# A one-core transformer block: the expert pipeline one chunk deeper, with four hidden banks and two banks for the rest

## What is computed

```python
h = _layernorm(x) * (1 + ca) + sa
x = x + ga * attn(h)                         # 16 heads of 128, causal
h = _layernorm(x) * (1 + cb) + sb
d = h @ down_w + down_b                      # 256 -> 128
gate, top = top 2 of softmax(h @ router_w + router_b - cost)
out = sum over k, e of gate_k * (gelu(gelu(d * mask_ke) @ w1_e + b1_e) @ w2_e + b2_e)
out = out + 0.1 * (gelu(gelu(d) @ shared_w1 + b) @ shared_w2 + b)
x = x + gb * (out @ up_w + up_b + gelu(h) @ core_w + core_b)
```

## Time and profile before

| | us |
|---|---|
| median of 3 runs | 826.7 (825.47 to 826.98) |
| profiled execution | 826.36 |
| its span, first to last instruction | 824.6 |
| PE busy | 791.6 (96%) |
| DVE busy | 681.7 (83%) |
| ACT busy | 626.6 (76%) |
| POOL busy | 441.8 (54%) |

### The profile page before, as it was taken

The page is one execution under the profiler, slowest core; times in us unless marked ns, Lnnn a source line. Parts: engine busy times, 40 slices in busy tenths (PEclk is TensorE's granted clock), DMA queues, the critical chain, the costliest instruction groups (busy, mean ns, idle before and its releaser), DMA issues.

```text
span 824.6 us, 14456 instructions
## 1 busy us (share of the span) xinstructions
PE 791.6 (96%) x4806; PEld 707.2 (86%) x4806; DVE 681.7 (83%) x1654; ACT 626.6 (76%) x1409; POOL 441.8 (54%) x306
## 2 busy tenths in 40 slices
PE   8899899999999999999999999999998788989997
PEld 7689898999999999999999999999998677768786
DVE  4789998888888888888888888889898898777876
ACT  3787878788778888778887788887778666677873
POOL 2555365644545566544566544675454364848554
PEclk8999999999999999999999999999999899999999
DMA  7263233442233433332233442244232220121121
GB/s 249 74 168 72 64 82 91 105 106 65 64 76 84 112 95 90 74 83 69 64 91 90 102 110 65 64 110 115 65 69 60 70 91 14 65 64 65 65 96 60
DMA packets 47594, 70.55 MB, mean 86 GB/s; under 512 B 5536, under 2 KB 38464, under 8 KB 47392
## 3 DMA queue, kind: packets, MB, share of 16 engines
q1 hardware_dynamic: 47008, 68.81, 31.4%
q0 software_dynamic: 368, 0.81, 0.3%
q10 hardware_dynamic: 144, 0.00, 0.0%
HBM read 25.49 MB, written 2.17 MB: 34 GB/s over the span
## 4 chain that ended last, share of the span: by engine, by line
PE 63%; ACT 15%; DVE 10%; issue 6%; POOL 4%; DMA 1%; POOLq 0%; SPq 0%; DVEq 0%; ACTq 0%
PE M L719 9%; PE M L720 9%; PE M L718 9%; PE T L718 6%; PE T L720 6%; PE T L719 6%; PE S L718 5%; PE S L720 5%; PE S L719 5%; ACT PB L613 4%; ACT PB L659 2%; DVE S L1115 2%; ACT pth L686 2%; ACT qk L672 2%; POOL stage L536 1%
## 5 line engine op out<-in xcount | busy, mean ns | idle before, releaser
L563 POOL TENSOR_TENSOR X<-X,fb 128x512 f32<-128x512 f32 x64 | 83.0, 1297 | 253.1 <-DVE fb L1149 253.1
L613 ACT ACTIVATE PB<-S,nb 128x128 f32<-128x128 f32 (+3 forms) x256 | 133.6, 532 | 109.5 <-DVE nb L1115 109.5
L570 POOL TENSOR_TENSOR ptl<-ptl,pth 128x640 fp32r<-128x640 f32 x127 | 198.4, 1583 | 32.9 <-ACT pth L686 32.9
L659 ACT ACTIVATE PB<-PB,ri 128x256 f32<-128x256 f32 (+3 forms) x256 | 124.5, 581 | 6.4 <-DVE ri L1124 6.3
L1115 DVE CUSTOM_DVE_ANT_0 S<-S,cc 128x128 f32<-128x128 f32 (+3 forms) x256 | 117.4, 521 | 1.3 <-PE S L720 1.3
L1100 DVE TENSOR_TENSOR qk<-M,qk 128x512 fp32r<-128x512 f32 x108 | 74.6, 690 | 45.5 <-ACT qk L672 45.5
L1131 DVE STREAM_TRANSPOSE gab<-PB 128x256 f32<-128x256 f32 (+2 forms) x192 | 109.4, 620 | 0.3 <-DMA ptl<-gab 0.3
L718 PE MATMUL S<-qk 128*128 128x128 f32 (+3 forms) x256 | 86.7, 339 | 4.7 <-DVE qk L1100 4.7
L686 ACT CAST pth<-ptl 128x640 fp32r<-128x640 f32 x128 | 87.8, 745 | 2.5 <-DMA ptl<-gab 2.5
L718 PE MATMUL M<-hh,W 128*128 128x512 f32 x222 | 87.3, 393 | 0.6 <-DVE hl L1086 0.6
L720 PE MATMUL M<-hh,W 128*128 128x512 f32 x222 | 87.4, 394 | 0.0
(11 more groups left out here) (236 smaller groups left out, 2431.5 us busy)
## 6 DMA issues: line engine op xcount, KB each, us to landing
ptl<-gab SPq DMA_DIRECT2D x256, 160.0 KB, 3.0
...
```

The source lines that it names most:

```text
L563: pool.tensor_tensor(X[:, a:a + 512], X[:, a:a + 512], fb[:, c2 * 512:c2 * 512 + 512], ALU.add).then_inc(s_y, 1)
L570: pool.tensor_tensor(ptl[u % 2][:, s], ptl[u % 2][:, s].bitcast(F32), pth[u % 2][:, s].bitcast(F32), ALU.subtract).then_inc(s_pl, 1)
L613: ins = act.activation(PB[:, P_OFF[i]:P_OFF[i] + w], PS[bk][:, a:a + w], ACT.Exp, bias=nb[:, i:i + 1], scale=-1.0, accum_out=sm[:, i:i + 1])
L659: act.activation(p, p, ACT.Copy, scale=ri[:, i:i + 1]).then_inc(s_P3, 1)
```

## The change

`LAG` goes from 3 to 4: w2(n) stands four steps behind w1(n). The hidden chunks take four banks (S0 to S2 and M2, `HID_AT`), and five buffers instead of four (`Gs`, the fifth in G4h and G4l); all other FFN results share M0 and M1. wo, r, z, h2, dn, dt, D and up therefore alternate between two banks. The tile wf goes, and its rows (`wF`) lie in fb, with waits for the transfer that reads them. P of unit 62 is split by DVE alone, P and z of unit 63 stand three and two steps later, behind router steps of batch 0 and r(1) (step 5 instead of 8). The normalization of batches 2 and 3 and its statistics stand one or more steps later, `dt` stands in step 21 instead of 18, the core inputs (`hs`, `gx`) three steps later in batches 1 to 3, `xb(t)` for t under 3 in step (t, 19) instead of (t + 1, 2).

```diff
...
 NC = sum(HID) // 128
 ORDER = [3, 2, 0, 1, 4, 5, 6, 7]
 PLACE = [n for n, e in enumerate(ORDER) for _ in range(HID[e] // 128)]
-LAG = 3
+LAG = 4
 FIRST_ACC = 6
 EULER = 2.718281828459045
 WARM = 60, 16, 12
...
     def put(t, j, *events):
         at.setdefault((t, j), []).extend(events)
 
-    put(0, 0, ("rs", 0, 3), ("rs", 0, 4), ("rs", 0, 5), ("rs", 0, 6))
-    put(0, 1, ("wo", last - 1, 0), ("rs", 0, 7), ("rs", 0, 8), ("rs", 0, 9))
-    put(0, 2, ("wo", last - 1, 1), ("pt", NU - 1))
-    put(0, 3, ("wh", 21), ("rs", 0, 10), ("rs", 0, 11))
-    put(0, 4, ("rs", 0, 12), ("rs", 0, 13), ("rs", 0, 14), ("wh", 22))
-    put(0, 5, ("z", NU - 1))
-    put(0, 6, ("wt", 0), ("wl", 0), ("wl", 1), ("wl", 2), ("st", 6, 0), ("st", 6, 1))
-    put(0, 7, ("wo", last, 0), ("st", 6, 2), ("st", 6, 3))
-    put(0, 8, ("wo", last, 1), ("wl", 3), ("d0", 0))
-    put(0, 9, ("nm", 6, 0), ("d0", 1))
-    put(0, 10, ("nm", 6, 1), ("d0", 2))
-    for k, j in enumerate((11, 12, 13, 13)):
+    put(0, 0, ("rs", 0, 3), ("rs", 0, 4), ("rs", 0, 5))
+    put(0, 1, ("wo", last - 1, 0), ("rs", 0, 6), ("rs", 0, 7))
+    put(0, 2, ("wo", last - 1, 1), ("rs", 0, 8), ("rs", 0, 9))
+    put(0, 3, ("wh", 21))
+    put(0, 4, ("rs", 0, 10), ("rs", 0, 11), ("rs", 0, 12))
+    put(0, 5, ("rs", 0, 13), ("rs", 0, 14), ("pt", NU - 1))
+    put(0, 6, ("wh", 22))
+    put(0, 7, ("wt", 0), ("wl", 0), ("wl", 1), ("wl", 2), ("z", NU - 1))
+    put(0, 8, ("st", 6, 0), ("st", 6, 1))
+    put(0, 9, ("wo", last, 0), ("st", 6, 2), ("st", 6, 3))
+    put(0, 10, ("wo", last, 1), ("wl", 3), ("nm", 6, 0))
+    put(0, 11, ("nm", 6, 1), ("d0", 0))
+    put(0, 12, ("h2", 2, 0), ("d0", 1))
+    put(0, 13, ("dn", 1), ("d0", 2))
+    put(0, 14, ("h2", 2, 1))
+    for k, j in enumerate((14, 15, 15, 16)):
         put(0, j, ("st", 7, k))
-    put(0, 12, ("h2", 2, 0))
-    put(0, 13, ("dn", 1))
-    put(0, 14, ("h2", 2, 1))
-    for c in range(3):
-        put(0, 15 + c, ("dta", c))
-    put(0, 15, ("nm", 7, 0))
-    put(0, 16, ("nm", 7, 1))
-    put(0, 18, ("dt",), ("h2", 3, 0))
-    put(0, 20, ("h2", 3, 1))
-    put(1, 0, ("hs", 0, 0))
-    put(1, 2, ("gx", 0, 0), ("hs", 0, 1))
-    put(1, 4, ("gx", 0, 1))
-    put(1, 6, ("D", 0))
-    for b, n in ((1, 8), (2, 22), (3, 43)):
+    put(0, 17, ("nm", 7, 0), ("dta", 0))
+    put(0, 18, ("nm", 7, 1), ("dta", 1))
+    put(0, 19, ("dta", 2), ("xb", 0))
+    put(0, 20, ("h2", 3, 0))
+    put(1, 0, ("dt",), ("h2", 3, 1))
+    put(1, 2, ("hs", 0, 0))
+    put(1, 4, ("gx", 0, 0), ("hs", 0, 1))
+    put(1, 6, ("gx", 0, 1), ("D", 0))
+    for b, n in ((1, 5), (2, 22), (3, 43)):
         def at_(i, *events):
             put(*divmod(i, NC + 1), *events)
         at_(n, ("r", b))
         at_(n + 1, ("rs", b, 1), ("rs", b, 2))
         for c in range(4):
             at_(n + 2 + c, ("rp", b, c))
-        if b == 1:
-            for k in range(3, 15):
-                at_(n + (6 + (k - 3) // 3 if k < 10 else 10 + (k - 10) // 3), ("rs", b, k))
-        else:
-            for k, m in enumerate((8, 8, 8, 11, 14, 14, 14, 17, 17, 17, 18, 18), 3):
-                at_(n + m, ("rs", b, k))
-        at_(n + (21 if b > 1 else 14), ("wt", b))
+        late = (8, 8, 8, 9, 11, 11, 11, 14, 14, 14, 15, 15) if b == 1 else (8, 8, 8, 11, 14, 14, 14, 17, 17, 17, 18, 18)
+        for k, m in enumerate(late, 3):
+            at_(n + m, ("rs", b, k))
+        at_(n + (21 if b > 1 else 17), ("wt", b))
     for t in range(1, B):
-        put(t, 2, ("xb", t - 1))
         put(t, 3, ("D", t))
-        put(t, 6, ("o", t - 1), ("hs", t, 0))
-        put(t, 8, ("gx", t, 0), ("hs", t, 1), ("up", t - 1, 0))
-        put(t, 10, ("gx", t, 1), ("up", t - 1, 1))
+        put(t, 6, ("o", t - 1))
+        put(t, 8, ("up", t - 1, 0))
+        put(t, 9, ("hs", t, 0))
+        put(t, 10, ("up", t - 1, 1))
+        put(t, 11, ("gx", t, 0), ("hs", t, 1))
+        put(t, 13, ("gx", t, 1))
         if t + 1 < B:
             put(t, 17, ("dn", t + 1))
+            put(t, 19, ("xb", t))
     put(B - 1, 18, ("xb", B - 1))
     chunks = B * (NC + 1)
     plan, later = [], []
...
     for n, ev in enumerate(plan):
         if ev[0] in MISC:
             use[ev] = len(use)
-            free = range(5 if n < len(attention) else 3)
+            free = range(5 if n < len(attention) else 2)
             bank_no[ev] = min(free, key=lambda k: use[last_of[k]] if k in last_of else -1)
             used_before[ev] = last_of.get(bank_no[ev])
             last_of[bank_no[ev]] = ev
...
         ebase = sb("ebase", 32)
         ru = sb("ru", 32, U32)
         g0 = sb("g0", 20 + 160)
+        sb("spare", 8)
         Dz = sb("Dz", 128, mybir.dt.bfloat16)
         Dm = sb("Dm", 128, F32R, parts=96)
         g0z = sb("g0z", 320, F32R)
...
             zt = sa("zt", 2048, F32R)
         ur = sb("ur", 2048, F32R)
         Gr = sb("Gr", 4096, F32R)
+        G4h = sb("G4h", 512, F32R)
         gob = sb("gob", 256)
         ol, oh = sb("ol", 512, F32R), sb("oh", 512, F32R)
+        wgw, G4l = sb("wgw", 512, F32R), sb("G4l", 512, F32R)
         prod = sb("prod", 1024)
-        wgw = sb("wgw", 512, F32R)
-        wf = sb("wf", 1024)
         gxh, gxl = sb("gxh", 2048, F32R), sb("gxl", 2048, F32R)
 
         PS = [ctx.enter_context(nc.psum_tensor(f"S{n}", [128, 512], F32)) for n in range(3)]
         PT = [ctx.enter_context(nc.psum_tensor(f"T{n}", [128, 512], F32)) for n in range(2)]
         M = [ctx.enter_context(nc.psum_tensor(f"M{n}", [128, 512], F32)) for n in range(3)]
+        HID_AT = PS + M[2:]
 
         ident = cc[:, C_ID:C_ID + 128]
         Yt = gab[:, 1024:2304]
...
             return stage[:, 1024 + (t % 2) * 512:1536 + (t % 2) * 512]
 
         def Gs(n):
-            o = (n + 2) % 4 * 1024
-            return Gr[:, o:o + 512], Gr[:, o + 512:o + 1024]
+            k = (n + 2) % 5
+            if k == 4:
+                return G4h[:], G4l[:]
+            return Gr[:, k * 1024:k * 1024 + 512], Gr[:, k * 1024 + 512:k * 1024 + 1024]
 
         def wb_at(i):
 
...
             return rows_r[0:96, (t % 2) * 512:512 + (t % 2) * 512]
 
         def wF(t):
-            return wf[0:8, (t % 2) * 512:512 + (t % 2) * 512]
+            return fb[0:8, 0:512]
 
         def xn_at(ev):
 
...
                                        ALU.add).then_inc(s_y, 1)
                 if ev[0] == "pt":
                     u = ev[1]
-                    for c in range(1 if u == NU - 2 else 2):
+                    for c in range(0 if u == NU - 2 else 2):
                         s = slice(640 * c, 640 * c + 640)
                         pool.wait_ge(s_ph, 2 * u + c + 1)
                         pool.tensor_tensor(ptl[u % 2][:, s], ptl[u % 2][:, s].bitcast(F32),
...
                     n = ev[1]
                     t, j = divmod(n, NC + 1)
                     bias = bc[:, B_SH1:B_SH1 + 1] if j == 0 else bc[:, B_B1 + j - 1:B_B1 + j]
-                    if n == 2:
+                    if n == 3:
                         act.wait_ge(s_ty, NU)
                     act.wait_ge(s_f1, n + 1)
-                    act.activation(Gs(n)[0], PS[n % 3][:], ACT.Gelu, bias=bias).then_inc(s_gh, 1)
-                    act.activation(PS[n % 3][:], PS[n % 3][:], ACT.Gelu, bias=bias).then_inc(s_v, 1)
+                    act.activation(Gs(n)[0], HID_AT[n % 4][:], ACT.Gelu, bias=bias).then_inc(s_gh, 1)
+                    act.activation(HID_AT[n % 4][:], HID_AT[n % 4][:], ACT.Gelu, bias=bias).then_inc(s_v, 1)
 
 
         @block.tensor
...
                     h = u % 4
                     pe.wait_ge(me, use[("v", u // 2, 1)] + 1)
                     va = (u // 2 % 2) * 1024 + (u % 2) * 128
-                    pe.wait_ge(s_pl, 2 * u + 2 - (u >= NU - 2))
                     if u == NU - 2:
-                        pe.wait_ge(s_pv, 1)
+                        pe.wait_ge(s_pv, 2)
+                    else:
+                        pe.wait_ge(s_pl, 2 * u + 2 - 2 * (u > NU - 2))
                     for j in range(4):
                         ins = mm3(o[:, 128 * j:512], (vh[:, va + 256 * j:va + 256 * j + 128],
                                                       vl[:, va + 256 * j:va + 256 * j + 128]),
...
                     t, j = divmod(n, NC + 1)
                     if j == 0:
                         pe.wait_ge(me, use[("dn", t)] + 1)
-                    if n >= 3:
-                        pe.wait_ge(s_gl, n - 2)
+                    if n >= 4:
+                        pe.wait_ge(s_gl, n - 3)
+                    elif n == 3:
+                        pe.wait_ge(me, use[last_of[2]] + 1)
                     else:
                         pe.wait_ge(s_E, 3 * NU)
                     a = F_SH1 if j == 0 else F_W1 + 128 * (j - 1)
-                    mm3(PS[n % 3][:], wt(0, a, 128), u_at(t), True, True).then_inc(s_f1, 1)
+                    mm3(HID_AT[n % 4][:], wt(0, a, 128), u_at(t), True, True).then_inc(s_f1, 1)
                 elif kind == "w2":
                     n = ev[1]
                     t, j = divmod(n, NC + 1)
...
```

(23 more changed lines are left out.)

## The result

The changed kernel takes 831.9 us (median of 5 runs, 830.3 to 834.5) where the kernel before takes 826.5 (824.8 to 827.0): a ratio of 1.0074, 95% interval 1.0052 to 1.0097. It is slower. The prediction said 824.6 and had 829.5 as its upper end, so it was wrong in sign and in range. The profiled execution took 831.92 us, with a span of 830.1 against 824.6.

A forecast was written before the change was run, and what follows sets the result against it. The prediction took PE and DVE, both close to full, to bound the first FFN stretch. Its terms summed to -1.9 us, 826.36 to 824.5 (median some 824.8); it put 824.6, range 818.5 to 829.5.

The forecast's parts named there:

- (A): P(62) wholly on DVE: z(62) starts earlier after a 1.4 us wait, clock stays full; -2.6 us.
- (E): dt two steps behind its inputs: its wait and slow clock go, h2(3,1), wt(1), r(2) wait instead; net -1.3 us.
- (H): Batch 1, xb(0) ahead of the powers, gx later: the 2.78 us wait becomes 1.25, slow clock goes; -3.3 us.
- (D): Steps 8 to 16: prod waits of 1.34, 1.20 and 0.44 us become 1.35, 0.75 and 2.8; +1.9 us.
- (J): The end: POOL's last addition, behind acc(3,6) and xb(3), ends the path; +0.65 us, up to +2 if the clock falls.
- everything else at nothing: Buffers placed anew, wF in fb and the product's waits were costed at nothing.
- (B): Two banks for the rest: wo(30,1) waits for the bank of z(62); +1.15 us.
- rival 2: Slower by bank hand-offs: two banks make PE wait at places before 700 us; +5.2 us, so 830; chance 0.20.
- (C): z(63) and P(63) later: PE waits 4.3 us at wt(0) for the router, before 4.39; -0.1 us, clock falls as before.
- rival 1: The bubbles close: the deeper ring lets DVE catch up, router steps slip between POOL's operations; 818 us; chance 0.25.
- (F): acc(0,8) stands behind D(1), not the core inputs gx(0,0): 1.99 us wait becomes 0.75; with small change -1.4 us.
- (I): Batches 2 and 3, same steps: waits of 0.69 and 0 become 1.25 each, accumulators before D(t) 0.75 each; +2.7 us.

The follow-up runs named there:

- e1: The changed kernel with xb(t) back in step (t+1, 2), all else as changed: 827.95 us, ratio 1.0029 to the kernel before.
- e7: e1 with LAG 3 in place of 4, all else as in e1: 821.01 us, ratio 0.9943 to the kernel before.
- e9: The changed kernel with LAG 3 in place of 4 and nothing else altered: 823.38 us, ratio 0.9971 to the kernel before.
- e3: The changed kernel without its eight unused columns (spare, 32 bytes per partition): 834.12 us, ratio 1.0097 to the kernel before.
- e6: e1 with hs and gx of batches 1 to 3 back in their old steps: 823.02 us, ratio 0.9963 to the kernel before.
- e5: e1 with xb(3) in step (3, 5) in place of (3, 18): 826.1 us, ratio 1.0003 to the kernel before.
- e2: The kernel before with only the eight unused columns (spare, 32 bytes) put ahead of Dz: 824.84 us, ratio 0.9991.

## Why the prediction was wrong

The sum was -1.9 us; the profiled executions give 831.92 - 826.36 = +5.6, so 7.5 us are to be explained. Two steps of the prediction failed. The first is the clock: (A), (E) and (H) booked 1.5 + 2.0 + 1.6 = 5.1 us of slow clock as removed, and (D) and (J) have no fall of the clock in their sums for the waits that they add. The runs showed that the sum of slow clock up to 820 us stayed at 6.8, and that the end lost 1.5 more: 6.6 us. The second is "everything else at nothing": 2.4 us of waits behind xb(1) and xb(2), and by the estimate above 2.5 in the pace of the FFN. Against these 11.5 stand the part in front, 2.3 us shorter, and waits that came out shorter than the prediction had them. Under both lies a premise that failed too: that a distance of two steps costs the same "whatever LAG is", so that the depth has no price. The runs showed 7.1 us (e1 against e7) and 8.5 us (after against e9) for it, most of that through the same waits and the same clock.

In the parts below, a wait from the timeline is some 0.15 us less than the same loss read from start to start, as the prediction often reads it (1.19 in the earlier trace rows is its 1.34).

**(A)** Held: a wait of 1.30 where 1.4 was said, at 632.58, with a granted clock of 1.00 in that stretch.

**(B)** 0.70 measured, 1.15 said. Waits released by the reads of banks M are 0.70, 0.61, 0.83 and 0.17, in sum 2.3 us, where rival 2 needed over 7. **(C)** The mechanism held: wt(0) waits, released by the router, and z(63) right behind it doesn't wait for P(63). It is 3.51 us in place of 4.3, and the clock falls behind it, as said. Rival 1 needed under 2 us here. So by its own signs neither rival came, and yet the time lies outside both.

**(D)** The three waits were said to be 1.35, 0.75 and 2.8 us: measured are 0.88, none and 2.27. In sum that is 3.15 against 2.52 in the kernel before (1.19, 1.05 and 0.28): +0.6, not +1.9. But the clock fell behind the 2.27 (0.90 and 0.93 in two stretches that had 1.00), another 1.7 us. With it the term comes out at +2.3, near the +1.9 said, by luck. The prediction had itself read that the clock fell behind a wait of 2.31, and priced no fall behind its 2.8. That is the first mistake of method: a wait was priced without its clock where it was added, and with it where it was removed. The fall isn't certain either: in e3 (2.33 us) and e6 (2.29) the same wait has 1.00 on both sides of it.

**(E)** h2(3,1), wt(1) and r(2) waited 0.61, 0.83 and 0.17 where 1.25, 1.4 and 0.3 were said. Yet the clock, said to stay, fell further than before, to 0.76 and 0.90 (0.83 and 1.00 before). It falls within the router's products of 16 columns (timeline of PE, after):

```profile
694.79 0.26 PE L845 MATMUL M<-W,hh 128*128 128x16 f32 x1
...
695.01 0.26 PE L845 MATMUL M<-W,hh 128*128 128x16 f32 x1
...
695.32 0.36 PE L845 MATMUL M<-W,hh 128*128 128x16 f32 x1
...
695.75 0.36 PE L845 MATMUL M<-W,hh 128*128 128x16 f32 x1
```

From 0.22 us for two matmuls it goes to 0.43, behind no wait over 0.83 us. Before the fall PE had three short waits and the narrow matmuls. So "no long wait, no fall" was the step that failed. The two stretches lose 3.4 us, (1 - 0.76 + 1 - 0.90) x 10, where the kernel before loses 1.7 and a gain of 2.0 was booked. What makes it fall stays open. The narrow matmuls alone don't: those of r(1), from 644.25 to 645.95 behind a wait of 0.70 at 639.22, kept 0.22 to their end, with a clock of 1.00.

**(F)** 1.99 us became none over 0.3, better than said. **(G)** 0.74 us, 0.5 said. **(H)** Right in batch 1: 1.01 and 0.55 us in place of 2.78, and no fall of the clock. **(I)** 1.01 in batches 2 and 3 where 1.25 was said. Of the accumulators before D(t), said to cost 0.75 each, batch 2 has 0.42 and batch 3 none; in their place stands a second wait of 0.53 behind gx in each batch, which no term names. The sum was near by luck. The e6 run shows what (H) and (I) miss: these waits come from the new place of gx, and it was avoidable.

**(J)** POOL set the end as said, but the wait is 2.00 in place of 1.15 us (the row of the kernel before follows), and the clock fell: 0.85 + 1.5 = +2.4, above even the longer end of +2.

```profile
816.95 0.38 PE L718 MATMUL M<-W,oh 128*128 128x256 f32 x1 [1.15 <-DVE ol L1238]
```

POOL's last addition behind xb(3) in the kernel after, and DVE behind it:

```profile
815.31 2.40 POOL L594 TENSOR_TENSOR X<-X,gob 128x1024 f32<-128x1024 f32 x1
817.67 1.29 POOL L539 TENSOR_TENSOR stage<-stage,prod 128x512 f32<-128x512 f32 x1
```

```profile
819.16 0.42 DVE L1246 TENSOR_TENSOR prod<-T,gab 128x256 f32<-128x256 f32 x1 [1.81 <-POOL stage L539]
```

By e5 only 0.25 us of the 2.00 is xb(3)'s; the rest is the chain of DVE's product, POOL's addition and DVE again. At lag 3 it leaves a wait of 1.05 (e9).

**"Everything else at nothing"** was wrong twice. The spare costs an estimated 2.5 us in the FFN (e2, e3), and gives about as much in attention. And xb(1) and xb(2), whose move to (t,19) the prediction didn't follow (it followed xb(0) alone), collided with the router's last steps: 2.4 us of waits, 3.7 us by e1. The earlier trace rows had the very mechanism. The Trainium skill, page "SBUF — State Buffer", section "Who interferes with whom", says that a DVE instruction with two SBUF inputs contends with a GpSimd instruction that reads SBUF, and one that takes at most one input from there, outside certain modes, doesn't. The trace agrees: 1.79 us for the operation on two SBUF operands, 0.67 for the one that reads PSUM. Of the powers it was the row that held: in the kernel after, a power of 1.64 us on POOL at 664.14 lay over two normalizations on DVE at 664.36 of 0.73 together, and (D)'s waits came out short, not 3 us long. The two next to them, at 666.40 beside a POOL addition, took 1.10. The row reads one small SBUF tile and couldn't decide it alone; a subtract on two SBUF tiles of 512 columns does: 0.69 us at 708.75 within three powers (707.21, 5.51 us), 1.73 at 724.32 beside additions.

**The depth.** The waits that the prediction names for the new order sum to 23.3 us ((A) to (J): 1.4 + 1.15 + 4.3 + 4.9 + 2.95 + 0.75 + 0.5 + 1.25 + 4.0 + 2.15). Measured in the FFN part are 20.7, and without wt(2) and wt(3) 18.3. So the walk along the queues was good to some 20%, on the long side, and part of that is the way of reading. What it never asked is what the same order would do at lag 3, so it couldn't see that the depth made none of the gains and much of the loss. At a given event PE has one w2 less behind it at lag 4, and nothing more ready. For wt(0) this can be read: PE comes to it 19.4 us after the last reciprocal at lag 4 (652.52 - 3.51 - 629.57), and 20.1 at lag 3 (653.24 - 2.16 - 630.98). The 0.7 is one triplet. DVE has wgw ready 22.95 and 22.26 us after it, so the other half of the 1.35 us is in DVE's queue. Behind the shorter wait of 2.16 the clock didn't fall in e9 (1.00 from 650 to 660, where after has 0.83). The Trainium skill, page "Perfetto Trace Analysis", section "Optimization Strategy", says that a gap repeating on the busy engine can mean too few buffers. Here it didn't: the repeated waits were for accumulators, of which there stayed two, and the ring of hidden tiles made deeper cost 7.1 to 8.5 us (e7, e9). The prediction argued this against rival 1, rightly, but gave the depth itself no price. The forecast of -1.9 us is near the 2.4 us that e9 gains at lag 3, but that is another kernel, with other waits.

Still open: why 32 bytes change the pace, and in opposite directions in the two parts; what makes the clock fall behind one wait and not behind another of the same length; the last 1.4 us of the balance; and whether the depth would cost as much in the old order of events, which wasn't tried.

## What to carry to other kernels

A deeper pipeline isn't free where every other event keeps its place: here it moved the fixed events one triplet nearer to PE's arrival and took cover away, so set the depth back by itself before you believe in it. Price a wait that you add with the clock that it may take, as you price one that you remove, and don't count on the clock where PE has several short waits and narrow matmuls in a row. Follow a moved POOL addition in every batch, not in the first alone, and ask which small DVE operations on two SBUF tiles lie beside it.

## What the runs showed of the chip

- 32 bytes in the place of the tiles behind `g0` change the pace of three 512-column matmuls from 0.687 to 0.702 us in the FFN and from 0.690 to 0.680 in attention; the operands hh and W of the latter weren't moved. With ur, Gr and G4h moved back it is 0.692 to 0.695.
- The granted clock fell from 2.4 to 1.2 GHz (two matmuls in 0.22 us became two in 0.43) behind waits of no more than 0.83 us, within matmuls of 16 columns (after); within another run of them, r(1), it stayed. The length of a wait alone doesn't settle it: the clock stayed behind waits of 2.16 us (e9), 2.29 (e6) and 2.33 (e3), and fell behind one of 2.27 (after).
- A DVE subtract of 512 columns on two SBUF tiles took 0.69 us within POOL powers and 1.73 beside POOL additions (after).
